# Cross-attention prepared within self-attention's last rounds, and LayerNorms cut otherwise

## What is computed

```python
x = x + self_attn(layernorm(x), ...)        # x: 16 batches x 128 rows x 256
x = x + cross_attn(layernorm(x), ctx, ctx)  # ctx: 16 x 128 x 256
x = x + moe(layernorm(x), ...)              # 64 experts, 8 of them per row, and a shared one

def cross_attn(q, k, v):                    # heads over rows: 8 heads of 16 rows
    qh, kh, vh = (t.reshape(b * 8, 16, -1) for t in (q, k, v))
    sm = softmax(einsum('bdm,bdn->bmn', qh, kh) / 4, axis=-1)
    return einsum('bmn,bcn->bcm', sm, vh).reshape(b, 128, 256)
```

## Time and profile before

| | us |
|---|---|
| median of 3 runs | 1217.5 (1216.9 to 1219.61) |
| profiled execution | 1218.7, its span 1216.9, mean granted clock 0.944 |
| TensorE busy | 1095.8 (90%) |
| POOL, VectorE, ScalarE busy | 621.2, 606.6, 566.1 |
| DMA | 96.92 MB, mean 80 GB/s |

### The profile page before, as it was taken

How to read it: one execution, slowest core, us unless ns; L and a number is a source line. 1 busy time by engine, 2 the same in 40 slices (tenths; PEclk the granted TensorE clock), 3 DMA queues, 4 the chain that set the end, 5 groups by cost and what they waited for, 6 DMA issues and landing times.

```text
span 1216.9 us, 22759 instructions
## 1 busy us (share of the span) xinstructions
PE 1095.8 (90%) x7471; PEld 898.7 (74%) x7504; DVE 606.6 (50%) x1342; ACT 566.1 (47%) x1185; POOL 621.2 (51%) x755
## 2 busy tenths in 40 slices
PE   5969999999999838989767999999999999999996
PEld 3747777776767626666456888888887888888886
DVE  5756777777777547777471332233233322332232
ACT  3426666666666516776543333333332333333332
POOL 3765656565665142210004666666665666566663
PEclk8968999999999958999858999999999999999998
DMA  5201101010101046663005344344344334344341
GB/s 127 62 1 27 28 24 30 22 29 24 28 25 28 18 100 152 144 142 92 1 14 133 99 115 114 97 121 108 103 121 126 105 107 121 98 113 116 96 119 56
DMA packets 74961, 96.92 MB, mean 80 GB/s; under 512 B 20412, under 2 KB 55868, under 8 KB 74892
## 3 DMA queue, kind: packets, MB, share of 16 engines
q1 hardware_dynamic: 74892, 96.05, 30.3%
HBM read 82.73 MB, written 13.12 MB: 79 GB/s over the span
## 4 chain that ended last, share of the span: by engine, by line
PE 57%; DVE 3%; issue 3%; ACT 1%; DMA 1%; POOL 0%; SPq 0%; POOLq 0%; DVEq 0%; ACTq 0%
PE bank L1608 29%; PE bank L1620 15%; PE bank L1277 3%; PE bank L1263 3%; PE bank L1309 3%; DVE xmax L1408 1%; PE bank L1320 1%; PE bank L1288 1%; DMA comb<-combine_scratch 0%; DVE X L1820 0%; PE bank L1295 0%; PE bank L1326 0%; DVE keys_x L1437 0%; PE bank L1583 0%; PE bank L1593 0%
## 5 line engine op out<-in xcount | busy, mean ns | idle before, releaser
L1834 POOL TENSOR_TENSOR hidden<-act_u,comb 128x512 f32<-128x512 f32 x132 | 217.7, 1649 | 215.0 <-DVE act_u L1802 143.9
L1802 DVE TENSOR_TENSOR act_u<-act_g,bank 128x512 f32<-128x512 f32 x132 | 90.8, 688 | 394.0 <-PE bank L1608 365.4
L1708 ACT ACTIVATE act_g<-bank 128x512 f32<-128x512 f32 x132 | 78.9, 598 | 356.6 <-PE bank L1608 356.6
L1608 PE MATMUL bank<-x_hi,up_hi 128*128 128x512 f32 x528 | 209.2, 396 | 5.8 <-POOL up_lo L1839 5.8
L1608 PE MATMUL bank<-x_lo,up_hi 128*128 128x512 f32 x528 | 208.3, 394 | 0.0
L1608 PE MATMUL bank<-x_hi,up_lo 128*128 128x512 f32 x528 | 206.6, 391 | 0.0
L833 ACT ACTIVATE probs<-bank 128x512 f32<-128x512 f32 x192 | 113.8, 604 | 81.9 <-PE bank L656 45.1
L1620 PE MATMUL bank<-down_hi,h_hi 128*128 128x256 f32 x528 | 149.3, 283 | 1.8 <-POOL down_lo L1844 1.8
L1620 PE MATMUL bank<-down_hi,h_lo 128*128 128x256 f32 x528 | 150.0, 284 | 0.0
L1620 PE MATMUL bank<-down_lo,h_hi 128*128 128x256 f32 x528 | 149.9, 284 | 0.0
L1839 POOL TENSOR_TENSOR up_lo<-up_in,up_hi 128x512 fp32r<-128x512 f32 x66 | 85.0, 1288 | 87.6 <-ACT up_hi L1720 87.6
(11 more groups left out here) (258 smaller groups left out, 2180.9 us busy)
## 6 DMA issues: line engine op xcount, KB each, us to landing
comb<-combine_scratch SPq DMA_DIRECT2D x132, 256.0 KB, 3.8
up_in<-in_w_up SPq DMA_DIRECT2D x66, 256.0 KB, 3.5
down_in<-in_w_down SPq DMA_DIRECT2D x66, 128.0 KB, 3.7
keys_x<-key_rows_x SPq DMA_DIRECT2D x32, 192.0 KB, 3.3
key_rows_x<-ctx_hi SPq DMA_DIRECT2D x256, 16.0 KB, 1.5
query_x<-xq_rows_hi SPq DMA_DIRECT2D x64, 64.0 KB, 3.2
ctx_in<-in_ctx SPq DMA_DIRECT2D x16, 128.0 KB, 2.1
key_rows_x<-ctx_lo SPq DMA_DIRECT2D x128, 16.0 KB, 1.5
```

Of the source, the lines that this page charges most:

```text
L1608: last = nc.tensor.matmul(out[:], wp[p][:, c, s, :], xp[:, c, t:t + 512], start=k == 0, stop=k == 5)
L1708: nc.scalar.activation(act_g[h][:], GATE[h][:], ACT.Silu).then_inc(S(f"gated{h}"), 1)
L1802: nc.vector.tensor_tensor(act_u[h][:], act_g[h][:], UP[h][:], ALU.mult).then_inc(S(f"upped{h}"), 1)
L1834: nc.gpsimd.tensor_tensor(hidden[h][:], act_u[h][:], comb[p][:, 512 * h:512 * h + 512], ALU.mult)\
```

## The change

- LN_TURNS has six parts: the first LayerNorm in batches 0 to 3, 4 to 7 and 8 to 15, the second in 0 to 11 and 12 to 15. The part on VectorE is cut in two (ln_open, ln_close), with other work between.
- Self-attention's tiles are cleared ahead of compression. TensorE turns batch 0's queries and raw projections between the ck and cv products; the cv work on VectorE comes behind batch 0's first masked scores.
- The second LayerNorm's first part is opened in round 12 and closed in round 13, its ScalarE half behind round 12. The second part is opened ahead of cross step 0, on ScalarE ahead of step 1, closed ahead of step 2.
- Cross-attention's tiles lie over buffers that are dead earlier. POOL clears the query slots behind its last work for batch 15; VectorE fills key slots in round 15; the queries of batches 0 to 3 are normalised and split on POOL and ScalarE in rounds 15 and 16, out of tiles of earlier stages; the maxima of batch 0 are computed among the units of round 16, those of batch 1 ahead of step 0. ScalarE's high part is a copy of POOL's result rather than an activation on X.
- In the steps the maxima are turned at unit 2 rather than 0, the shift is kept at unit 3 rather than 0, and the next high part at unit 0 rather than 2. ctx_transposes stays at unit 3 with its wait.

The diff's core (helpers that are only moved out of a function, and the order of tiles in memory, are left out):

```diff
-LN_TURNS = ((0, 4), (4, 16), (0, 16), (0, 16))
+LN_TURNS = ((0, 4), (4, 8), (8, 16), (0, 12), (12, 16), (0, 16))
...
+        def ln_open(dve, n):
...
+        def ln_close(dve, n):
+            new = slice(*LN_TURNS[n - 1])
...
             dve.wait_ge(S("ld_x1"), 16)
             for b in range(4, 8):
                 batch_stats(b)
+            ln_open(dve, 2)
             normal(2)
             for b in range(8, 12):
                 batch_stats(b)
             normal(3)
+            ln_close(dve, 2)
+            normal(4)
             for b in range(12, B):
                 batch_stats(b)
-            ln_stats_vector(dve, 2)
+            ln_open(dve, 3)
...
             for b in range(B):
-                if b + 4 < B:
+                if b == 3:
+                    ln_close(dve, 3)
+                if b and b + 4 < B:
                     normal(b + 4)
...
             for b in range(B):
-                if b == 2:
-                    ln_stats_scalar(act, 2)
+                if b in (1, 3):
+                    ln_stats_scalar(act, 2 + b // 2)
                 keep_proj(b)
...
             last.then_inc(S("ck_done"), 1)
+            query_transposes(pe, 0)
+            raw_transposes(pe, 0)
             pe.wait_ge(S("hid_kept"), 8)
...
         def comp_vector(dve):
+            nc.vector.memset(imp[:], -1e30).then_inc(S("vector_steps"), 1)
+            dve.wait_ge(S("vector_steps"), 4)
+            nc.vector.memset(imp[:, :, NB:NB + 1], NO_BLOCK)
+            nc.vector.memset(blockmax[:], -1e30)
+            nc.vector.memset(farmax[:], -1e30).then_inc(S("attn_zeroed"), 1)
...
+        def comp_values_vector(dve):
             dve.wait_ge(S("cv_done"), 1)
...
             def block_scores(n):
                 pe.wait_ge(S("rawT_kept"), n + 1)
+                if n == 0:
+                    pe.wait_ge(S("ck_ready"), 2)
...
                 if u == 0:
+                    if b == 0:
+                        pe.wait_ge(S("attn_zeroed"), 2)
+                        pe.wait_ge(S("cv_ready"), 1)
...
                 if l:
                     values(b - 1, 5)
-                if n:
-                    raw_transposes(b + 1)
+                if q and n:
+                    raw_transposes(pe, b + 1)
                 for u in range(UNITS):
                     if q:
                         score(b, u)
-                    if u == 1 and n:
-                        query_transposes(b + 1)
+                    if u == 1 and q and n:
+                        query_transposes(pe, b + 1)
                     if u == 2 and n:
                         block_scores(b + 1)
+                    if b == B and u in (0, 2, 5, 9):
+                        for m in {0: (0, 1), 2: (2, 3), 5: (4, 5), 9: (6, 7)}[u]:
+                            cross_max_scores(pe, 0, m)
...
+                    if b == B - 1 and u in (9, 11):
+                        cross_query_high(act, (u - 9) // 2)
+                    if b == B and u in (0, 7):
+                        cross_query_high(act, 2 + u // 7)
                 if n:
                     rows_keep(b + 1)
+                if b == 12:
+                    ln_stats_scalar(act, 4)
...
             for b in BATCHES:
                 n, q, l = b + 1 < B, 0 <= b < B, b >= 1
                 if n:
                     comp_in(b + 1)
+                if b == -1:
+                    comp_values_vector(dve)
+                if b == B:
+                    cross_reduce_max(dve, 0, 0)
+                    cross_reduce_max(dve, 0, 1)
                 if l:
                     add_branch(b - 1, FINE)
+                if b == B - 1:
+                    cross_ones(dve, (0, 1, 2))
+                if b == B:
+                    cross_reduce_max(dve, 0, 2)
+                    cross_reduce_max(dve, 0, 3)
+                    cross_reduce_max(dve, 0, 4)
+                    cross_reduce_max(dve, 0, 5)
...
+                if b == 12:
+                    ln_open(dve, 4)
+                if b == 13:
+                    ln_close(dve, 4)
                 if q:
                     add_branch(b, WINDOW)
+                if b == B - 1:
+                    dve.wait_ge(S("cout_done"), B)
+                    cross_ones(dve, (3,))
+                if b == B:
+                    cross_reduce_max(dve, 0, 6)
+                    cross_reduce_max(dve, 0, 7)
...
             pool.wait_ge(S("attn_zeroed"), 2)
+            pool.wait_ge(S("proj_kept"), B)
             rotate(0)
...
+            cross_zero_queries(pool)
+            for b in range(4):
+                cross_query(pool, b)
+                if b:
+                    cross_query_low(pool, b - 1)
...
-        XSCORE = [bank[0], bank[1], bank[2]]
-        XMAX = [bank[3], bank[4]]
-        XPV, XOUT, XT = bank[5], bank[6], bank[7]
+        XSCORE = [bank[0], bank[1], bank[6]]
+        XMAX = [bank[2], bank[3]]
+        XPV, XT, XOUT = bank[4], bank[5], bank[7]
         MAX_ORDER = (0, 2, 1, 3)
-        STEPS = range(-4, B + 2)
...
-            sp.wait_ge(S("cross_zeroed"), 2)
             for p in range(2):
                 sp.wait_ge(S(f"ctx_out{p}"), 384 * (B // 2))
+            sp.wait_ge(S("keys_zeroed"), 1)
+            for b in range(2):
+                load_keys(b, b, b)
+            sp.wait_ge(S("query_zeroed"), 1)
...
-                    load_keys(b, p, s)
+                    if b == 3:
+                        sp.wait_ge(S("keys_zeroed"), 2)
+                    if b >= 2:
+                        load_keys(b, p, s)
...
+        def cross_query_high(act, b):
+            p = b % 2
+            if b >= 2:
+                act.wait_ge(S(f"xq_out{p}"), 32 * (b // 2))
+            else:
+                act.wait_ge(S(f"ctx_out{p}"), 384 * (B // 2))
+            act.wait_ge(S("xq_ready"), b + 1)
+            nc.scalar.copy(xq_hi[p][:], xq[p]).then_inc(S("xq_hi_ready"), 1)
+
...
+        def cross_zero_queries(pool):
+            pool.wait_ge(S("rawT_done"), B)
+            for s in range(4):
+                last = nc.gpsimd.memset(query_x[s][:].bitcast(F32), 0.0)
+            last.then_inc(S("query_zeroed"), 1)
+
+        def cross_ones(dve, slots):
+            for s in slots:
+                last = nc.vector.memset(keys_x[s][:].bitcast(F32), 1.0)
+            last.then_inc(S("keys_zeroed"), 1)
...
-            pe.wait_ge(S("cross_zeroed"), 2)
+            pe.wait_ge(S("cout_kept"), B)
+            pe.wait_ge(S("prob_ready"), UNITS * B)
+            shift_transposes(0)
+            for u in range(XH):
+                cross_max_scores(pe, 1, u)
+            pe.wait_ge(S("pv_kept"), 2 * B)
             pe.wait_ge(S("attn_added"), B)
-            for i in STEPS:
+            for i in range(B + 2):
                 for u in range(XH):
-                    if 0 <= i < B:
+                    if i < B:
                         score(i, u)
-                    if u == 0 and 0 <= i + 1 < B:
+                    if u == 2 and i + 1 < B:
                         shift_transposes(i + 1)
-                    if 0 <= i + 2 < B:
-                        max_scores(i + 2, u)
+                    if i + 2 < B:
+                        cross_max_scores(pe, i + 2, u)
                     if u == 1 and 0 <= i - 2 < B:
...
+            keep_shift(0)
+            for i in range(B + 2):
+                if i == 1:
+                    ln_stats_scalar(act, 5)
                 for u in range(XH):
-                    if 0 <= i < B:
+                    if i < B:
                         softmax(i, u)
-                    if u == 0 and 0 <= i + 1 < B:
+                    if u == 3 and i + 1 < B:
                         keep_shift(i + 1)
-                    if u == 2 and 0 <= i + 4 < B:
-                        query_high(i + 4)
+                    if u == 0 and i + 4 < B:
+                        cross_query_high(act, i + 4)
                     if u == 4 and 0 <= i < B:
                         keep_values(i)
...
-            dve.wait_ge(S("attn_added"), B)
             for p in range(2):
                 last = nc.vector.memset(xvalue[p][:], 0.0)
             last.then_inc(S("vector_steps"), 1)
             dve.wait_ge(S("vector_steps"), 7)
             for p in range(2):
-                nc.vector.memset(xvalue[p][:, :, :, XC:XC + 1], 1.0)
-            for s in range(4):
-                last = nc.vector.memset(keys_x[s][:].bitcast(F32), 1.0)
-            last.then_inc(S("cross_zeroed"), 1)
-            ln_stats_vector(dve, 3)
-            nc.vector.scalar_tensor_tensor(xbias[:], mean[:], -1.0, rstd[:], ALU.mult, ALU.mult)\
-                .then_inc(S("xbias_ready"), 1)
-            for i in STEPS:
+                last = nc.vector.memset(xvalue[p][:, :, :, XC:XC + 1], 1.0)
+            last.then_inc(S("xvalue_set"), 1)
+            for u in range(XH):
+                cross_reduce_max(dve, 1, u)
+            ln_open(dve, 5)
+            for i in range(B + 2):
+                if i == 2:
+                    ln_close(dve, 5)
                 for u in range(XH):
```

(8 more changed lines are left out.)

196 lines of the change are left out of this document (86 added, 110 removed).

## The result

| | us |
|---|---|
| before, median of 7 runs | 1217.5 (1215.2 to 1219.6) |
| after, median of 7 runs | 1213.9 (1210.6 to 1215.4) |
| ratio, 95% interval | 0.9968 (0.9956 to 0.9980) |
| profiled execution of after | 1215.4, its span 1213.4, mean granted clock 0.950 |

The kernel is faster by some 3.6 us, not by 12.7; the time lies at the slow end of the range on record (1196 to 1214). Five places are compared, each with rows of before.

What follows compares the result with a forecast made beforehand. TensorE was taken as the busiest engine, nearly the bound in cross steps, with idle holes at the passages. 7.5 - 2.1 + 12.3 - 5.0 = 12.7 us gained, 1206.0 from the profiled 1218.7, 1205 against the median; range 1196 to 1214.

Steps and rivals of the forecast that it cites:

- part 5: Cross steps, shift turned later: steps go from 8.43 to 8.7 us, 5.0 us lost; bounds 9 lost and 5 won.
- part 3: LayerNorm of batches 0 to 11 in round 12: round 13's first softmax 2.1 us late, all lost; bounds 0.5 and 3.
- part 2: Passage into self-attention: masked scores 5.3 us earlier, less the cv product in VectorE's queue, 3.9 us gained; bounds 2 and 6.
- part 4: Passage from self- to cross-attention: first score at 448.7 instead of 461.03, 12.3 us gained; bounds 9 and 15.
- Part 1: First LayerNorm in 4, 4, 8: batch 6's turn at about 27.0 instead of 30.64, 3.6 us gained; bounds 0.9 and 3.8.
- the block scores come when ck_sum is ready: Entry to self-attention: block scores wait only for ck_sum, so VectorE's first masked scores come at about 71.1, 5.3 us earlier.
- rival B: The front gives little: clock falls in shorter holes, VectorE becomes the bound; front 3, passage 10, time 1212; chance 0.15.
- The table loads: ScalarE's LayerNorms: 1.28 us per load, 3.0 us per Ln and Exp, without the skill's drain of about 1.38 us per switch.
- the context wait is hidden and a step falls to 8.0: Cross steps, favourable bound of the later shift: TensorE's wait before the context turn disappears, 5 us won.
- A: Rival for the cross steps: ScalarE gets to the shift before TensorE needs it; steps of 8.0 us, time 1195; chance 0.15.
- C: Rival, slower than before: the shift's transfer lands after the step's end, the next first score waits; 1221.5 us; chance 0.06.
- D: Rival for the passage: first queries ready no sooner than the tail's end; passage gives under 5 us, time 1212; chance 0.08.

Runs made afterwards that it cites:

- kernel 9: The changed kernel with 7 and 5 idle matmuls in TensorE's two front waits, ahead of compression and of batch 0's query turn: 1210.2 us.
- kernels 8 and 9: The first: the changed kernel with 14 and 10 idle matmuls in the two front waits, 1215.4 us; the second is kernel 9.
- kernel 7: The changed kernel with the cv product ahead of the turns of batch 0's queries and raw projections again: 1214.1 us.
- kernels 1 and 5: Both on the changed kernel. First: maxima turned at unit 0 again, its last part undone, 1202.8 us. Second: LayerNorm of batches 12 to 15 out of step 1, 1212.2 us.
- kernel 3: The changed kernel with only ScalarE's copy of the shift moved from unit 3 to unit 2: 1197.3 us.
- kernels 2 and 3: The first: the changed kernel with the context turn at unit 5 and its copy at unit 6, 1196.5 us; the second is kernel 3.

## Why the prediction was right in direction and wrong in size

The steps that failed are terms of the sum. Of the 9.9 us between 12.7 forecast and 2.8 in the profiles, part 5 has 5.4, part 3 has 2.9 and part 2 has 2.5; part 4 gives back 0.9. All three lie beyond their own bounds (9 lost, 3 lost, 2 won).

| part | forecast | profile | what the runs say |
|---|---|---|---|
| 1, LayerNorm 4, 4, 8 | +3.6 | +3.6 | +3.1 alone |
| 2, into self-attention | +3.9 | +1.4 | 3.7 more with the waits filled |
| 3, LayerNorm in round 12 | -2.1 | -5.0 | 2.9 more with the wait filled |
| 4, passage | +12.3 | +13.2 | |
| 5, shift turned later | -5.0 | -10.4 | -11.1 undone, -6.0 alone |
| together | 12.7 | 2.8 | 3.6 by the medians |

The spans differ by 3.5 us; the 0.7 beyond the 2.8 arise in the mixture of experts, and weren't looked into.

**Part 1** holds, by its own step: two short waits (0.78 and 0.88 us on L327), batch 6 at 27.07 where I had put 27.0, no fall of the clock.

**Part 2.** Forecast was the first masked score at 71.1; it came at 74.1. The step that failed is "the block scores come when ck_sum is ready". ck_sum was ready at 68.9 (67.08 + 1.80), but TensorE, which now has the turns and the cv product ahead of them, came to the block scores at 71.90. Behind its wait of 1.32 us for the rotation the raw turns took 1.91 us and the cv product 3.58, at a granted clock of 0.50 from 66 on; at full clock, in kernel 9, they take 1.03 and 2.03. Half clock behind a wait was nothing new for the raw turns (2.04 us in the earlier trace rows, behind 4.27 us of waiting), but the cv product had run ahead of that wait at full clock (2.03 us), and nothing in the sum prices the two in one slow stretch. The cv product in VectorE's queue cost 1.0 us and not 1.5 (with which the sum would be 5.3 - 1.5 = 3.8, not 3.9): the lead is 5.92 us at the masked scores and 4.94 at the turn of the first shift rows (91.38 against 86.44). The front's two kernels 8 and 9 show that it is the clock; kernel 7 shows that the order alone doesn't mend it.

**Part 3.** The mechanism and its 2 us are right: the softmax came at 364.58, 2.04 us late, and TensorE stood 1.88 us. The mis-sized term is what follows a wait: another 3.0 us at the lower level in this execution, 1.5 or none in others; with it the part is beyond my upper bound of 3 (and by the average of the ten profiles, 2.0 + 1.2 us, just beyond it). I had weighed the fall of the clock in part 1 and in rival B, not here, where the earlier trace rows shows nothing but full clock; but no round of it had such a wait of TensorE.

The table loads took 1.28 us and the next operation came 0.02 us after, in both places: Ln, Exp and their loads 3.0 us, as the sum had it. The Trainium skill (ScalarE: Activation LUTs, What ACT_TABLE_LOAD costs) adds a drain of 1.38 us per switch; by it the softmax would have come an estimated 2.8 us later than it did, so the trace doesn't agree.

**Part 4** is right step by step (as round 14 begins the lead is 0, so the axes can be compared as they stand): first maxima 429.1 (forecast 428.4), residual 439.4 (439.5), first score 447.8 (448.7).

**Part 5.** The mechanism was the one forecast: the step's own stall goes, and a wait of 0.80 us (forecast 0.9) for ScalarE's copy takes its place. Two terms were too small. The step: 8.97 us, not 8.7; the context turn comes 5.26 us into it, not 5.05. Half of that is a slip in the sum: by its own terms unit 3's score stands at 4.19 - 0.84 + 0.4 = +3.75 and not at +3.6, and it came at +3.72 (505.92, in a step that begins at 502.20). So softmax and copy are each some 0.1 us later than worked out; the context turn follows the copy's end (+5.11) by 0.15 us, not 0.05, and behind it another 0.04 is lost. Over 13 steps that is 0.54 x 13 = 7.0 in place of 3.9. And step 1: I gave it 1.1 us; it lost 3, as the late copy, the LayerNorm and the clock act on each other. With the late shift or the LayerNorm gone (kernels 1 and 5) the step is of ordinary length; in kernel 3, with both there but the copy earlier, it is still 1.8 us over the others (451.24 to 461.00). The forecast's own bound, "the context wait is hidden and a step falls to 8.0", is what kernels 2 and 3 are.

**The rivals.** A (the shift pays) didn't happen, but two units' distance or one moved line makes it happen. B's cause, the clock behind shorter holes, is what cut part 2 (and part 3, where B had not placed it); the passage gave its full 12 to 13. C (the shift's transfer lands late) didn't happen: no score waits for it. D neither. The number of B and D, 1212, came nearest, and by luck: the front gave 5.0 us where B had 3, the passage its full gain, and what was lost was lost in round 13 and the steps.

## What to carry to other kernels

A wait removed on one engine is worth what the next consumer of the moved result allows: list everything that waits for that semaphore, and look where in the producer's in-order queue the work stands. Here moving the copy of the shift ahead of a softmax whose input comes later turned a loss of 11 us into a gain of 5 (1197.3 against 1202.8 with the old order). Cost a new wait of TensorE, even of 1.3 to 1.9 us, at both prices, with and without a stretch at half clock behind it, and where it can't be avoided, try idle matmuls that last no longer than it does. One profile shows one outcome of the clock; compare several before a loss is called the change's.

## What the runs showed of the hardware that I had not expected

- A wait of 1.88 us of TensorE, in a stretch at 2.4 GHz, was followed by some 6.7 us mostly at 1.2 GHz (0.55 from 365 to 370 us) and cost 3.0 us beyond itself; one of 1.35 us was followed by 4 us at 0.57, and in all seven profiles that have it that step takes 10.2 to 11.8 us, against 9.0 for the others. With matmuls in the wait (0.44 us of it left) the clock stayed full in all three profiles.
- It isn't certain: the same 1.88 us left the clock full in five of ten profiles. Behind the same wait of 1.86 us compression took 7.19 us in four and 8.88 in six. The Trainium skill (TensorE: Matmul & The Clock Gate, The HAM clock gate) says that the number of slow matmuls at the start of one kernel varies between its runs, with the clock gate's phase at that start. These counts show such a variation in the middle of a kernel; no run here shows its cause.
- In kernel 7 the clock fell inside the cv product (32 products of 8 columns) with no wait ahead of it: 2.86 us, where it took 2.03 before. Which property of that stretch does it isn't settled.
- Each fp32 product is two matmuls in the trace: 22 of 256 columns are 44, and took 9.76 us, 0.44 each.
